# A graph network on one Trainium2 core: values of the attention stage leave the gather ring by a DMA of SyncE in place of ScalarE's copy

## The reference

```python
q = einsum('ni,hid->nhd', x, Wq) + bq; k = ... Wk; v = ... Wv
e = edge_attr[:, None, None] * We[None, :, :]
alpha = einsum('ehd,ehd->eh', q[dst], k[src] + e) / sqrt(d)
ex = exp(alpha - segment_max(alpha, dst)[dst])
w = ex / segment_sum(ex, dst)[dst]
agg = segment_sum(w[:, :, None] * (v[src] + e), dst)
out = layernorm((agg + skip) @ Wo + bo + x)
```

## Time and profile before

| | before |
|---|---|
| median of 3 runs | 6020.16 us |
| the profiled execution's own time | 6009.66 us |
| its span, first to last instruction | 6007.6 us |
| mean granted TensorE clock | 0.778 |
| attention stage, roughly | 130 to 1420 us of the span |
| engines' busy share over the span | POOL 71%, PE 65%, DVE 61%, ACT 47% |

### The profile page before, as it was taken

The page is one execution under the profiler, slowest core; times in us unless marked ns, Lnnn a source line. Parts: engine busy times, 40 slices in busy tenths (PEclk is TensorE's granted clock), DMA queues, the critical chain, the costliest instruction groups (busy, mean ns, idle before and its releaser), DMA issues. The chain is left out here.

```text
span 6007.6 us, 92656 instructions
## 1 busy us (share of the span) xinstructions
PE 3885.8 (65%) x20652; PEld 3141.3 (52%) x20652; DVE 3669.8 (61%) x11763; ACT 2801.3 (47%) x6925; POOL 4295.4 (71%) x4477
## 2 busy tenths in 40 slices
PE   5577777775766776678888887444344346666665
PEld 5466666664555555545655655333333346664443
DVE  6788888886988888666777765111011034445665
ACT  3688888882211111145555654111111158884444
POOL 2677777763777777767777777777777767777775
PEclk8788878887999888878888887555555579898887
DMA  4444444453755555622333325333233245552223
GB/s 125 121 136 131 130 131 129 128 116 101 200 149 145 149 148 148 127 65 74 74 77 74 75 73 100 83 79 78 78 79 78 70 133 168 165 166 79 58 57 45
DMA packets 485359, 652.55 MB, mean 109 GB/s; under 512 B 119512, under 2 KB 332245, under 8 KB 484822
## 3 DMA queue, kind: packets, MB, share of 16 engines
q0 software_dynamic: 155552, 349.05, 23.3%
q1 hardware_dynamic: 329271, 297.58, 18.8%
HBM read 495.44 MB, written 150.71 MB: 108 GB/s over the span
## 5 line engine op out<-in xcount | busy, mean ns | idle before, releaser
L694 POOL DMA_INDIRECT kv_ring<-keys_values,gather_i x880 | 862.2, 980 | 348.9 <-issue 258.4
L694 POOL DMA_INDIRECT arena<-table,gather_i x880 | 856.4, 973 | 291.1 <-issue 266.4
L694 POOL DMA_INDIRECT e_ring<-filter_rows,gather_i x880 | 841.8, 957 | 299.8 <-issue 267.9
L2221 POOL DMA_INDIRECT rows_by_src<-arena,key x880 | 858.3, 975 | 268.7 <-issue 267.6
L694 POOL DMA_INDIRECT e_ring<-table,gather_i x880 | 844.5, 960 | 275.0 <-issue 264.8
L2133 PE MATMUL e_pt<-nodes,arena 128*128 x1728 | 442.5, 437 | 628.5 <-ACT arena L2142 620.9
L2133 PEld LDWEIGHTS e_pt<-nodes,arena 128*128 128x128 f32 x1728 | 381.2, 325 | 690.3 <-issue 690.3
L2125 DVE TENSOR_SCALAR arena<-arena,part 128x512 f32<-128x512 bf16 x220 | 115.2, 525 | 913.1 <-PE e_pt L2133 910.9
L2376 PE MATMUL gl_sum_f<-arena,gl_hot_f 128*128 128x128 f32 x1760 | 282.6, 310 | 446.0 <-DMA arena<-table,gather_i 173.9
L1582 PE MATMUL e_pa<-e_msg,e_hot 128*128 128x128 f32 x3520 | 543.9, 305 | 30.5 <-DVE e_msg L1803 22.7
L743 DVE TENSOR_TENSOR arena<-arena,e_pa 128x128 f32 x1760 | 497.4, 283 | 99.9 <-PE e_pa L1582 70.5
(11 more groups left out here) (463 smaller groups left out, 9784.5 us busy)
## 6 DMA issues: line engine op xcount, KB each, us to landing
rows_by_src<-e_filler SPq DMA_DIRECT2D x256, 260.0 KB
arena<-rows_by_src SPq DMA_DIRECT2D x256, 260.0 KB, 2.9
at_rows<-local_rows SPq DMA_DIRECT2D x220, 128.0 KB, 3.5
e_rows<-local_rows SPq DMA_DIRECT2D x220, 128.0 KB
arena<-local_rows SPq DMA_DIRECT2D x220, 128.0 KB
e_attr<-edge_attr SPq DMA_DIRECT2D x880, 25.0 KB
kv_ring<-keys_values,gather_i POOLq DMA_INDIRECT x880
e_ring<-table,gather_i POOLq DMA_INDIRECT x880
```

The source lines that it names most:

```text
L694: pool.indirect_dma_start(ring[:, r, u, :], None, table, bass.IndirectOffsetOnAxis(index, 0)).then_inc(arrived[r], 16)
L2221: pool.indirect_dma_start(self.table, bass.IndirectOffsetOnAxis(place, 0), self.out[:, r, u, :], None)\
```

## The change

`keep_values` moves from ScalarE's list into SyncE's. What was an activation (copy) of 128 x 512 floats within the on-chip memory is now a DMA between the same two places, 128 partitions x 4 pieces of 512 bytes, 256 KB. It is issued in loop step k of SyncE for batch k - 5, behind the load of the rows of batch k and ahead of the load of the run breaks. It waits for the same two conditions, and it signals one semaphore for each ring slot (`valued0` to `valued5`) by 16 in place of one common semaphore by 1. The wait in GpSimd's gathers and the one in VectorE's `message` follow. Since values are also kept for the last batches, SyncE's loop does it up to step 224, past the last rows.

```diff
--- before.py
+++ after.py
@@ -822,7 +822,7 @@
 
         arrived, rows_in, pens_in = c.kv_arrived, [sem(f"rows{r}") for r in range(R)], [sem(f"pens{r}") for r in range(2)]
         hots_t, queried, producted, weighed, reduced = (sem(n) for n in ("hots_t", "queried", "producted", "weighed", "reduced"))
-        lasts, linked, start, valued = (sem(n) for n in ("lasts", "linked", "start", "valued"))
+        lasts, linked, start, valued = sem("lasts"), sem("linked"), sem("start"), [sem(f"valued{r}") for r in range(KR)]
         scored, turned, scanned, rowed, spread, walked, backed, carried = (sem(n) for n in ("scored", "turned", "scanned", "rowed", "spread", "walked", "backed", "carried"))
         maxed, returned, shifted, fallen, exped = (sem(n) for n in ("maxed", "returned", "shifted", "fallen", "exped"))
         ranked, rescaled = sem("ranked"), sem("rescaled")
@@ -836,7 +836,13 @@
 
         @block.gpsimd
         def _(pool):
-            gather_rows(pool, c, c.kv, ring, arrived, [(producted, 1), (valued, 1)], range(KR, BATCHES))
+            for k in range(KR, BATCHES):
+                r = k % KR
+                pool.wait_ge(producted, k - KR + 1)
+                pool.wait_ge(valued[r], 16 * (k // KR))
+                for u in range(U):
+                    index = c.gather_i[:, k * U + u:k * U + u + 1]
+                    pool.indirect_dma_start(ring[:, r, u, :], None, c.kv, bass.IndirectOffsetOnAxis(index, 0)).then_inc(arrived[r], 16)
 
         @block.sync
         def _(sp):
@@ -849,6 +855,12 @@
                 at = bucket_in_turn(nc, c, n, SP_ENGINE)
                 sp.wait_ge(taken, node_reads_before(NODE_AT[n] + PROJECTED + 1))
                 sp.dma_start(c.table3[bass.ds(at, 1), :, :].rearrange("one p f -> p (one f)"), rows_out[:, n % 2, :]).then_inc(row_sent[n % 2], 16)
+
+            def keep_values(k):
+                r = k % KR
+                sp.wait_ge(arrived[r], 16 * U * (k // KR + 1))
+                at_least(sp, messages, k - VALS + 1, None)
+                sp.dma_start(values[:, k % VALS, :, :], ring[:, r, :, F:2 * F]).then_inc(valued[r], 16)
 
             sp.dma_start(last, c.key[P - 1:P, :]).then_inc(lasts, 16)
             for to, of in small_weights:
@@ -861,10 +873,13 @@
                 n = node_due(k, PROJECTED + 4)
                 if n is not None:
                     send_rows(n)
+                if k < BATCHES:
+                    at_least(sp, hots_t, 2 * (k - R + 1), None)
+                    load_local_rows(sp, c, rows, k, k % R, rows_in)
+                if 0 <= k - 5 < BATCHES:
+                    keep_values(k - 5)
                 if k >= BATCHES:
                     continue
-                at_least(sp, hots_t, 2 * (k - R + 1), None)
-                load_local_rows(sp, c, rows, k, k % R, rows_in)
                 if k % CB == CB - 1:
                     n = k // CB
                     if n == 0:
@@ -1014,12 +1029,6 @@
                 act.wait_ge(hots, 5 * k + 4)
                 act.activation(to, to, ACT.Relu, bias=c.ones[:, 0:1], scale=-1.0).then_inc(hots, 1)
 
-            def keep_values(k):
-                r = k % KR
-                act.wait_ge(arrived[r], 16 * U * (k // KR + 1))
-                at_least(act, messages, k - VALS + 1, None)
-                act.activation(values[:, k % VALS, :, :], ring[:, r, :, F:2 * F], ACT.Copy).then_inc(valued, 1)
-
             def exps(k):
                 n, at = k // CB, k % CB * U
                 act.wait_ge(exped, 3 * n + 1)
@@ -1090,8 +1099,6 @@
                         inverse_root(node_due(s, lag + 1), w)
                 if ph == 1 and 0 <= n - 1 < CHUNKS:
                     exponents(n - 1)
-                if 0 <= s - 1 < BATCHES:
-                    keep_values(s - 1)
                 if 0 <= s - LAG < BATCHES:
                     exps(s - LAG)
                 if ph == 1 and 0 <= n < CHUNKS:
@@ -1202,7 +1209,7 @@
 
             def message(k):
                 q, n, at = k % 2, k // CB, k % CB * U
-                dve.wait_ge(valued, k + 1)
+                dve.wait_ge(valued[k % KR], 16 * (k // KR + 1))
                 dve.tensor_tensor(msg[:, q, :, 0:F].rearrange("p u (h d) -> p u h d", d=D),
                                   ex[:, n % 2, :, at:at + U].rearrange("p h u -> p u h").unsqueeze(3).broadcast_to([P, U, H, D]),
                                   values[:, k % VALS, :, :].rearrange("p u (h d) -> p u h d", d=D), ALU.mult).then_inc(messages, 1)
```

## The result

The changed kernel takes 6037.86 us, the median of 7 runs (6034.01 to 6042.66), beside 6023.98 us of the kernel before on the same chip (7 runs, 6014.58 to 6030.21). The ratio is 1.0027, with a 95% interval of 1.0018 to 1.0037: slower by 14 us, where 6014 was forecast. It lies above the range. The profiled execution took 6042.35 us, its span 6040.3 us.

The account below looks back on a forecast made before the run. The prediction took VectorE to set the attention stage's pace. From the median 6020.2 us it took 6 us for the removed copies and added 0 for contention, latency and issue, giving 6014, range 6002 to 6031.

Parts of the forecast that it names:

- VectorE sets the pace: Attention stage, 200 to 1330 us: VectorE is the bound, 86% busy, with TensorE following and ScalarE having some slack.
- The copies' gain, 6 us: ScalarE: removing 220 copies shortens 10 of 25 waits of TensorE and VectorE, 6 us; bound from above 15.3 us.
- GpSimd's 58.4 us, worth nothing: Gathers' waits for ScalarE's copy: ending them gains nothing, since GpSimd is ahead and the ring of six is full.
- the 1.0 that I allowed: SyncE's list: issuing a values DMA of 512 pieces may hold SyncE for 1.0 us, within its spare time.
- I cost contention at nothing: DMA engines: share rising from 0.48 to 0.65 costs nothing, unless gathers slow by over 0.10 us each.
- VectorE's list is the same: VectorE: the change leaves its list of work as it was; no cost was put on it.
- Slower by contention: Rival: DMA contention slows each gather and its gap by 0.13 us, the ring empties, 21 us slower, 6041; chance 0.11.
- ScalarE as the bound: Rival: ScalarE was the bound after all, so the kernel gets 24 us faster, 5996; chance 0.15.
- SyncE's queue being late: Rival: rows behind a held-up values DMA make ScalarE wait, 0.5 us per run break, 27 us slower, 6047; chance 0.06.
- The prediction's 2.6 us for a landing: Values DMA: estimate from the skill page, 2.0 us plus bytes over 436 GB/s; the prediction itself took 3 us.

Follow-up runs that it names:

- moving one line: Kernel before, with VectorE's load of four bucket numbers moved from ahead of the products to right behind them: 5956.17 us, ratio 0.9892.
- the experiment without traffic: Changed kernel with values moved for the first ten batches alone, later messages reading old values: 6023.08 us, ratio 0.9996.
- the spare DMA: Kernel before, ScalarE's copy kept, plus a 256 KB DMA a batch from SyncE into unused memory, in 512-byte pieces: 6039.2 us against 6023.71.
- the two kernels with the load moved: Kernel before and changed kernel, each with VectorE's load of four bucket numbers moved behind the products: 5956.17 us and 5968.11 us.
- the two kernels without loads: Kernel before and changed kernel, each with VectorE's and TensorE's four bucket numbers replaced by a constant: 5954.62 us and 5956.98 us.
- Both spare DMAs: Kernel before plus 256 KB a batch within on-chip memory, in 512 pieces of 512 bytes or 128 of 2048: 6039.2 us and 6036.85 us.
- the same kernel with two batches in a load: Kernel before, with VectorE loading eight bucket numbers for two batches every second slot: 6007.24 us against 6024.02, ratio 0.9974.

## Why the prediction was wrong

**VectorE sets the pace: right.** Its idle time is what became longer, and what is taken off its path comes off the time (64 us by moving one line).

**The copies' gain, 6 us: not confirmed.** The copies left ScalarE, 118 us of busy time in the stretch, and its waits for others took their place. The term measured 0.6 us, in the experiment without traffic, with an interval of about 5 us around it, which does not exclude 6. The rows speak for the small value: waits of TensorE for ScalarE went from 33.5 to 31.4 us, and VectorE's for the exponentials stayed at 5.5.

**GpSimd's 58.4 us, worth nothing: right**, since the ring stayed full. The new order, the semaphores, the waits in SyncE's list and the missing copies were not measured one by one; together they cost nothing that shows, since the whole change costs 14 us and the spare DMA, without them, 15.5. The issue of a values DMA takes 0.607 us in the median, not the 1.0 that I allowed.

**"I cost contention at nothing": the step that failed.** It was read from the gathers alone. Their part was right: 979 ns, even 974 at a share of 0.78, and the ring stayed full. But I had taken "VectorE's list is the same" to mean that VectorE's time is the same. Its instructions are, yet its sequencer reads registers from memory between them, 4 numbers a batch, and those reads lengthened with traffic: 352 to 512 ns. They stood in no row that I read, since the profile counts them as not busy; they appear as idle time "issue" ahead of the products, which I called "between its own instructions" and left unopened. The spare DMA measured the term by itself, 6039.2 - 6023.7 = 15.5 us: the sum 6020.2 - 0.6 + 15.5 lands at 6035, 3 us from the time. Of the 24 us by which the forecast missed, 3.8 are the base, 6020.16 us of 3 runs then and 6023.98 of 7 now.

**The rivals.** Slower by contention was among them, but through gathers that slow, with a price of 21 us and a chance of 0.11. The sign and nearly the size came true, the mechanism did not. ScalarE as the bound is excluded by the experiment without traffic, which has no copy and is not faster by the 24 us of that rival. SyncE's queue being late is not tested there, since the values DMAs and their waits are gone with the traffic; against it stand the spare DMA, which costs as much without those waits, and the rows: no wait of ScalarE for `at_rows` stands among them.

**The rule of the Trainium skill** that spoke against the change (DMA: Bandwidth & Descriptors, section "Issuing engines are not separate DMA queues") says that DMAs run on the same 16 engines and interleave. The trace agrees that the values DMAs take a share of them, 0.63 in place of 0.48, but the gathers kept their 979 ns, so the loss did not come by that rule. Another page of the Trainium skill (SBUF — State Buffer, section "Who interferes with whom") says that a DMA never contends with a compute engine. For the engine's instructions the runs agree, 688 ns a product. For the register loads of its sequencer, which that section does not mention, the rule can't be relied on: they lengthened from 352 to 512 ns, and the measurement decides. The prediction's 2.6 us for a landing rest on the Trainium skill's fit for DMAs that GpSimd issues (DMA: Bandwidth & Descriptors, section "Anatomy of one DMA — SWDGE (gpsimd) path"); the values DMA is SyncE's, and no trace here tells when it lands.

**What stays open.** TensorE's register loads lengthen too (the mean of all of them from 0.396 to 0.473 us between the two kernels with the load moved). What that costs was not measured by itself; the two kernels without loads can't tell, since the gathers pace them. The small rest of the slot's growth that does not stand behind VectorE's loads is open as well. By which path loads and DMAs meet is not shown either. Both spare DMAs read and write on-chip memory, so whether traffic to DRAM alone does the same wasn't tried.

## What to carry to other kernels

Before calling an engine's list unchanged, read what its sequencer does between the instructions; idle time marked "issue" on the engine that sets the pace is worth opening, and here most of it was register loads, worth more than the change. Put a register load behind a long instruction and ahead of the place that needs it, not behind a short one. Here a copy taken from an engine with slack to the DMA engines gained nothing measurable and added traffic; where the slack is real, leave it there. The version to keep here is the kernel before with one line moved, 5956.17 us, which beats both kernels.

## What was unexpected in the hardware

- Between batches 40 and 210 of the kernel before, a register load of four numbers from on-chip memory took 0.35 us in the median and 0.445 in the mean, and in the same kernel with two batches in a load, one of eight took 0.82 and 0.775.
- With DMA traffic going from 131 to 176 GB/s, VectorE's median load of four numbers went from 352 to 422, 479 or 512 ns in three kernels, and the longest from 0.60 us to between 1.24 and 1.30; at 219 GB/s it was 561 ns and 1.41 us. SyncE's load of one number went from 458 to 724 ns. TensorE's median hardly moved (336 to 339 ns) until 219 GB/s, where it was 508.
- A gather's mean stayed between 973 and 989 ns in all twelve kernels, and that of a product between 685 and 689 ns.
